# A six-cell attention stage in one kernel: pairing heads in the value product, output weights reordered in DRAM, input normalised in place

## The chip, the cores and the metric

The kernel runs on one core of one Trainium2 chip. Its time is the device time of one execution in microseconds (us): median 3191.99 us of three runs (3191.54 to 3194.13). The profiled execution took 3187.25 us, of which the span from first to last instruction is 3185.5 us, at a mean granted TensorE clock of 0.981 of full speed.

## The reference, cut to what matters

The reference is a chain of six residual layers on x of shape (64, 64, 256), that is 4096 tokens in 64 sequences of 64 tokens. Only the third layer, here called the cell stage, is changed. For the normalised input and for each of six nodes c it computes

```
nodes = {-1: inputs}
for c in range(6):
    q = ew[c, 0] * (nodes[c - 1]   @ We[eq] + be[eq])
    k = ew[c, 1] * (nodes[in_k]    @ We[ek] + be[ek])
    v = ew[c, 2] * (nodes[in_v]    @ We[ev] + be[ev])
    o = _mha(q, k, v, Wq[c], Wk[c], Wv[c], Wo[c])      # 8 heads of 32, softmax over the 64 tokens of a sequence
    nodes[c] = act_w[c] * o + q
out = _layernorm(nodes[5], ln_g, ln_b)                  # added to x
```

`_mha` projects q, k and v with 256x256 matrices, splits them into 8 heads of 32 columns, and multiplies the joined heads by Wo.

## The kernel before, in words

`build` runs the stages one after the other: masked attention, wide attention, the cell stage (`stage_cell`, about 1650 to 2733 us of the span), attention over a context, a scan, a feed-forward stage. Each stage gives every engine (PE, ACT, DVE, POOL, SP) its own list of instructions, written by hand, and semaphores join the lists. Nothing is scheduled at run time: each engine works through its list in order.

The cell stage has two parts.

*Preparation* (1650 to about 1717 us). Edge matrix and projection matrix of every node are multiplied once, because `(x @ We) @ Wq` is `x @ (We @ Wq)`. SP loads raw matrices (`load_raw`, L1939) into buffers that the main part uses later: even nodes into `prob`, odd ones into `probT` and `v`. For each of the 18 pairs (node c, f = q, k or v) PE transposes We (L2015), ACT copies it out (L2260), PE computes the bias column (L2022: four products of 128x128 by one column), then the fused matrix (L2030), and DVE scales it (L2438). SP waits for a node's last product before it loads the raw matrices two nodes ahead (L1957), and stores finished sets to DRAM (L1962). ACT loads the first edge and output matrix at n = 4 (`load_own`, L2243).

*Main part.* Tokens are worked on in blocks of 512; a round handles two blocks, X = 0 and 1, and there are four rounds (`rounds`, L1926: the first and last are written out, the middle two are a loop). A round has 12 slots: nodes c = 0 to 5 for X = 0 and 1. So the stage has 48 slots. A slot of PE's list (`body`, L2187) is: half of the q edge product (`add_edge`, L2133), turning the later two heads' probabilities (L2116), the other half, the value product `attend` (L2144), the next node's k projection (L2059), the output product `add_output` (L2155), turning the next slot's first two heads' probabilities (L2108), v projection (L2082), q projection (L2059), scores (L2097). In the slots of c = 5 the k projection is replaced by transposing the next round's input (`turn_input`, L2048), and the projections follow later. ACT copies results out of PSUM, applies exp; DVE finds maxima, sums and divisions, and makes the low parts for the split products (fp32r products are made three times, high by high, high by low, low by high).

`attend` (L2136) before: heads are numbered hf*4 + r, hf = 0 or 1, r = 0 to 3. Partitions 0 to 63 of `probT` hold the keys of the heads of hf = 0, partitions 64 to 127 those of hf = 1, and `v` is stored the same way: [128, X, s, b, 128 columns]. For each of the 8 sequences of a block (s, b), each hf and each r there is one fp32 product: 64 keys by 32 value columns as stationary operand, 64 query columns as moving operand. That is 64 products, in the array tiles of 64 rows by 32 columns. Results of hf go to bank `ring[hf]`, and the semaphore `attended` is raised for hf = 0 and hf = 1 after the last sequence. ACT then writes the high part of `oT` (L2353) and DVE the low part (L2537, a helper at L2419), one bank after the other; `add_output` waits for the first bank's low part, makes six products, waits for the second's (L2152).

`normalise` (L2407) waits for the input block in `x_ln`, makes statistics (DVE, L102), reciprocal roots (POOL, L114) and writes the normalised block into `xn[X]` (L130). One buffer `x_ln` serves all blocks; SP loads the next one when the last was read (L1979). POOL does nothing else in the stage than the roots. PE's two records for one fp32 product are both called MATMUL in the trace; an fp32r product or a transpose has one.

Of the kernel before, what the change touches and what calls it, by code (L numbers as in the profile page):

```python
# [1736 lines left out]
def stage_cell(nc, mem, const, x_in, ew, act_w, W_e, b_e, W_q, W_k, W_v, W_o, ln_g, ln_b, x_out):  # L1737
# [49 lines left out]
    set_dram = nc.dram_tensor("cell_weights", (NODES, P, 3 * MAT), F32, kind="Internal").ap()  # L1787
    w_stage = mem.sb("w_stage", [P, SET])
# [11 lines left out]
    x_ln = mem.sb("x_ln", [P, SUB, D])  # L1800
# [4 lines left out]
    v = mem.sb("v", [P, 2, SUB, 2, P])  # L1805
# [22 lines left out]
    set_loaded = mem.sem("set_loaded")  # L1828
    set_hi = mem.sem("set_hi")
# [11 lines left out]
    x_loaded = mem.sem("x_loaded")  # L1841
# [42 lines left out]

    def set_number(i, c):

        return i * NODES + c + 1
# [29 lines left out]

    def attention(i, c, X):

        return i * (2 * NODES) + 2 * c + X  # L1920
# [17 lines left out]
    def _(sp):  # L1938
# [25 lines left out]
        sp.wait_ge(norm.xn_ready, 1)  # L1964
        sp.dma_start(x_ln[:, :, :], block_rows(x_in[BLK:2 * BLK, :])).then_inc(x_loaded, 16)

        def body(i, last):
            for X in range(2):
                if not isinstance(i, int) or i >= 1:

                    sp.wait_ge(y_stored[X], i * 16)
                elif X == 0:

                    sp.wait_ge(stage_stored[1], STORED)
                sp.dma_start(x_res[:, X], block_rows(x_in[rows((i * 2 + X) * BLK, BLK), :])).then_inc(res_loaded[X], 16)
            if not last:
                for X in range(2):

                    sp.wait_ge(norm.xn_ready, (i + 1) * 2 + X)  # L1979
                    sp.dma_start(x_ln[:, :, :], block_rows(x_in[rows(((i + 1) * 2 + X) * BLK, BLK), :])).then_inc(x_loaded, 16)  # L1980
# [3 lines left out]
    @block.gpsimd  # L1984
    def _(pool):
        for X in range(2):
            norm.gpsimd_rstd(pool, X)

        def body(i, last):
            for X in range(2):  # L1990
                if not last:
                    norm.gpsimd_rstd(pool, (i + 1) * 2 + X)
            for X in range(2):
                last_norm.gpsimd_rstd(pool, i * 2 + X)

        rounds(pool, body)

    @block.tensor
    def _(pe):
# [6 lines left out]
        for c in range(NODES):  # L2006
            for f in range(3):
# [11 lines left out]
                for oh in range(DH):  # L2019
                    at = n * DH + oh  # L2020
                    for mh in range(DH):
                        mm = pe.matmul(prep_banks[3][:, at:at + 1], raw_w(c, RAW_W + f)[:, mh, oh * P:(oh + 1) * P],  # L2022
                                       be[:, mh, edge[c][f]:edge[c][f] + 1], start=(mh == 0), stop=(mh == DH - 1))
# [218 lines left out]
    def _(act):  # L2242
        def load_own(c):  # L2243

            for at, w in ((EDGE_AT, W_e[edge[c][0]]), (OUT_AT, W_o[c])):
                act.dma_start(w_stage[:, at:at + MAT].rearrange("p (h o) -> p h o", h=DH), w.rearrange("(h p) o -> p h o", p=P)).then_inc(set_loaded, 16)
# [64 lines left out]
        act.wait_ge(stage_stored[1], STORED)  # L2311
        copy_v(DH, 0)
# [93 lines left out]
    def _(dve):  # L2406
        def normalise(blk, X, turned):  # L2407
            dve.wait_ge(x_loaded, (blk + 1) * 16)
            norm.vector_stats(dve, blk, x_ln)
# [3 lines left out]
            norm.vector_apply(dve, blk, x_ln, False, xn[:, X])  # L2413
# [108 lines left out]
        def body(i, last):  # L2522
            for c, X in slots():
# [34 lines left out]
                if c in (3, 4) and X == 0 and not last:  # L2558
                    Y = c - 3

                    turned = Y * 6 + DH if isinstance(i, int) and i == 0 else proj_at(i, NODES - 1, Y) - PROJ_ROUND + DH
                    normalise((i + 1) * 2 + Y, Y, turned)
# [803 lines left out]
```

## Time and profile before

| | |
|---|---|
| Median of 3 runs | 3191.99 us |
| Profiled execution | 3187.25 us (span 3185.5 us) |
| PE busy, whole span | 3017.8 us (95%) |
| DVE / ACT / POOL busy | 2186.4 (69%) / 2009.2 (63%) / 941.1 (30%) us |
| Cell stage | about 1650 to 2733 us of the span |

The profile's page names busy shares, and the trace answers questions on a stretch, on a line, on waits. "Busy" counts the time in which at least one record of the engine is open; matmuls are pipelined, so their records overlap, and the mean duration of one is not what one costs. What one costs is read from the starts: the start of a group of instructions to the start of the next group on the engine.

### The profile page before, as it was taken

To read this page: it belongs to the slowest core of one execution; us is meant where nothing else is said; L and a number is where in the kernel's file an instruction comes from. 1 tells how busy PE (TensorE), PEld (TensorE's weight loads), DVE (VectorE), ACT (ScalarE), POOL (GpSimd) and SP (SyncE) were. 2 spreads that over 40 slices of the span, in tenths; PEclk is the share of its full clock that TensorE was granted. 3 is DMA by queue.
4 is the path that set the end of the run, shared out by engine and by line. 5 is a ranking of instruction groups with operands and counts; after the bars stand their busy time and mean duration, and the time that the engine had idled before them with its cause. 6 is when DMAs were issued, how large, how long until landed. Compare 5 with 4: busy or idle time off the path is not lost. (4 is left out here: it accounts for less than half of the span.)

```text
span 3185.5 us, 88343 instructions
## 1 busy us (share of the span) xinstructions
PE 3017.8 (95%) x34369; PEld 2466.6 (77%) x34369; DVE 2186.4 (69%) x5188; ACT 2009.2 (63%) x3697; POOL 941.1 (30%) x812
## 2 busy tenths in 40 slices
PE   8999999979999999999979999999999999799999
PEld 7888888857877877877868888788788787564798
DVE  5777777766666666666644788778778877567543
ACT  5777777757767767677743677676666766332444
POOL 3444444337656555555630000000000000111210
PEclk9999999989999999999989999999999999899899
DMA  2111111237888888888885111111111110552000
GB/s 86 47 46 46 46 46 46 57 52 128 151 141 150 151 137 146 152 145 148 156 188 173 35 42 49 55 42 49 56 42 42 54 36 19 179 163 77 7 21 27
DMA packets 643036, 273.37 MB, mean 86 GB/s; under 512 B 549387, under 2 KB 617952, under 8 KB 642736
## 3 DMA queue, kind: packets, MB, share of 16 engines
q1 hardware_dynamic: 613168, 225.13, 33.6%
q10 hardware_dynamic: 29568, 44.05, 4.2%
q8 instruction: 212, 3.47, 0.5%
q14 instruction: 88, 0.72, 0.1%
HBM read 113.37 MB, written 21.50 MB: 42 GB/s over the span
## 5 line engine op out<-in xcount | busy, mean ns | idle before, releaser
L1310 POOL TENSOR_TENSOR front_parts<-wide_prob,front_parts 128x1024 f16<-128x1024 f32 x256 | 549.1, 2146 | 377.5 <-ACT front_parts L1536 318.6
L1629 DVE TENSOR_REDUCE wide_row_max<-wide_score 128x1 f32<-128x1024 f32 x256 | 312.6, 1221 | 167.4 <-PE wide_score L1348 166.5
L1348 PE MATMUL wide_score<-wide_kT,wide_qT 128*128 128x512 f32 x1536 | 414.3, 405 | 4.9 <-ACT wide_prob L1524 3.3
L1524 ACT ACTIVATE wide_prob<-wide_score,wide_neg_max 128x1024 f32<-128x1024 f32 x256 | 285.2, 1114 | 157.3 <-DVE wide_neg_max L1632 151.0
L886 ACT ACTIVATE mask_prob<-mask_prob,mask_row_min 128x256 f32<-128x256 f32 x512 | 232.0, 503 | 161.7 <-DVE mask_row_min L966 161.7
L1348 PEld LDWEIGHTS wide_score<-wide_kT,wide_qT 128*128 128x128 f32 x1536 | 277.5, 190 | 66.0 <-issue 8.9
L1536 ACT ACTIVATE front_parts<-wide_prob 128x1024 f16<-128x1024 f32 x256 | 269.8, 1054 | 16.8 <-ACT wide_prob L1524 8.3
L2472 DVE TENSOR_REDUCE cell_row_max<-cell_score 128x8 f32<-128x512 f32 x192 | 131.0, 682 | 148.5 <-PE cell_score L2097 146.6
L117 POOL TENSOR_TENSOR cell_var_eps<-cell_mean_var,const_eps 128x4 f32<-128x4 f32 x8 | 1.6, 202 | 651.9 <-DVE cell_mean_var L111 651.9
L1364 PE MATMUL wide_turn<-front_probT,wide_v 128*128 128x256 f16 x1536 | 189.5, 273 | 2.5 <-DMA front_probT<-front_parts 2.5
L1364 PE MATMUL wide_pv<-front_probT,wide_v 128*128 128x256 f16 x1536 | 189.9, 273 | 0.5 <-DMA front_probT<-front_parts 0.5
L966 DVE CUSTOM_DVE_ANT_0 mask_prob<-mask_score,mask_shut 128x256 f32<-128x256 f32 x512 | 188.0, 419 | 0.0
L1364 PEld LDWEIGHTS wide_turn<-front_probT,wide_v 128*128 128x128 f16 x1536 | 140.6, 98 | 50.0 <-issue 35.6
L1364 PEld LDWEIGHTS wide_pv<-front_probT,wide_v 128*128 128x128 f16 x1536 | 140.4, 98 | 47.3 <-issue 32.6
L2133 PE MATMUL cell_acc<-cell_node,cell_w 128*128 128x512 f32 x576 | 159.8, 413 | 13.2 <-issue 7.0
L2300 ACT ACTIVATE cell_v<-cell_score 64x256 f32<-64x256 f32 x384 | 145.5, 379 | 35.6 <-PE cell_score L2082 25.5
L752 PE MATMUL mask_turn<-const_ident,mask_prob 128*128 128x128 f32 x1024 | 157.2, 276 | 9.7 <-ACT mask_probT L894 9.4
L1623 DVE SCALAR_TENSOR_TENSOR front_x_all<-wide_misc,wide_inv_sum,front_x_all 128x256 f32<-128x256 f32 (+1 forms) x256 | 112.0, 478 | 68.9 <-PE wide_misc L1375 68.9
L2082 PE MATMUL cell_score<-cell_w,cell_node 128*128 128x256 f32 x1152 | 151.3, 288 | 5.5 <-DVE cell_node L2419 4.0
L2155 PE MATMUL cell_acc<-cell_oT,cell_w 128*128 128x512 f32 x576 | 145.7, 402 | 10.8 <-DVE cell_oT L2419 10.8
L2082 PEld LDWEIGHTS cell_score<-cell_w,cell_node 128*128 128x128 f32 x1152 | 142.6, 193 | 9.4 <-issue 5.7
L2059 PE MATMUL cell_score<-cell_node,cell_w 128*128 128x512 f32 x576 | 147.1, 402 | 1.7 <-DVE cell_prob L2475 1.7
(364 smaller groups left out, 6845.6 us busy)
## 6 DMA issues: line engine op xcount, KB each, us to landing
cell_w_stage<-cell_weights ACTq DMA_DIRECT2D x24, 768.0 KB, 6.1
mask_ctx<-in_ctx SPq DMA_DIRECT2D x32, 512.0 KB, 3.9
ctx_ctx<-in_ctx SPq DMA_DIRECT2D x32, 512.0 KB, 4.2
mask_mask<-in_mask_BxS_ik SPq DMA_DIRECT2D x32, 256.0 KB, 4.0
front_probT<-front_parts SPq DMA_TRANSPOSE x512, 3.2
cell_w_stage<-in_L_ffn_We ACTq DMA_DIRECT2D x24, 256.0 KB, 2.7
cell_w_stage<-in_L_ffn_Wo ACTq DMA_DIRECT2D x24, 256.0 KB, 3.1
front_x_all<-in_x SPq DMA_DIRECT2D x32, 128.0 KB, 2.0
```

The costliest lines, as they stand in the source:

```text
L752: mm = pe.transpose(turn[:, (i * KT + kt) * P:(i * KT + kt + 1) * P], prob[:, b, s * 2 + i, kt * P:(kt + 1) * P], ident[:, :])
L886: ins = act.activation(prob[:, b, p, :], prob[:, b, p, :], ACT.Exp, bias=row_min[:, b, p:p + 1], scale=-1.0)
L966: ins = dve.tensor_tensor_reduce(prob[:, b, p, :], score[p % ROW][:, p // ROW * CTX:(p // ROW + 1) * CTX], shut[:, k, b].rearrange("p t r ...
L1310: pool.tensor_tensor(parts[:, s % 2, LO, :], prob[:, s % 2, :], parts[:, s % 2, HI, :], ALU.subtract).then_inc(part_lo, 1)
L1348: mm = pe.matmul(score[:, s % 2, half * 512:(half + 1) * 512], qT[:, u_par, a, s * P:(s + 1) * P], kT[:, par, b, half * 512:(half + 1) * 5 ...
L1364: mm = pe.matmul(pv_banks[hf][:, :], v[:, par, a, kb, :], probT[:, u_par, hf, :, b, kb, :], start=(kb == 0 and i == 0), stop=(kb == KB - 1 ...
L1524: act.activation(prob[:, s % 2, :], score[:, s % 2, :], ACT.Exp, bias=neg_max[:, s % 2:s % 2 + 1], scale=SHARP, accum_out=row_sum[:, u_par ...
L1536: act.activation(parts[:, s % 2, HI, :], prob[:, s % 2, :], ACT.Copy).then_inc(part_hi, 1)
L1629: dve.tensor_reduce(row_max[:, one], score[:, s % 2, :], AX.X, ALU.max).then_inc(max_found, 1)
L2059: mm = pe.matmul(dst[:, :], weight(a, fused_at(f), ih, half(oh)), src[:, b, ih, :], start=(j == 0 and ih == 0), stop=(j == 2 and ih == DH ...
L2082: mm = pe.matmul(score[2 + pair][:, s * D:(s + 1) * D], v_src[:, a, ih, half(2 * pair + s)], weight(b, fused_at(2), ih, slice(0, D)), star ...
L2133: pe.matmul(acc[oh][:, :], weight(a_, EDGE_AT, ih, half(oh)), src[:, b_, ih, :], start=(j == 0 and ih == 0), stop=False)
```

## The change

- `attend` makes one product for two heads, r of hf = 0 and r of hf = 1: 128 keys (partitions 0 to 127, both halves) by 64 value columns, 64 query columns. `v` gets 256 columns per sequence, in blocks of 64 for each r: 32 columns of hf = 0, then 32 of hf = 1. In the rows of one half the columns of the other are zero. There are 32 products, in array tiles of 128 rows by 64 columns. r = 0, 1 go to `ring[0]`, r = 2, 3 to `ring[1]`; all of bank 0 comes first, and `attended` is raised in the middle and at the end.
- POOL clears the zero places of `v` by four memsets, each waiting for the one before, once the last raw matrix in `v` has been used; ACT's first copy into `v` waits for them.
- The rows of `oT` now have another order. `W_o` is copied in DRAM to `out_dram` in that order, by 24 DMAs from DRAM to DRAM (`regroup_out`), 4 of them before the raw loads of node 1 and 20 behind them, in SP's list. `load_own` reads `out_dram`. The v bias columns are made in the new order, by 16 products of 32 columns instead of 4 of 128, for each of the 6 nodes.
- `x_ln` is gone: blocks are loaded into `xn[X]` and normalised there. The load of a round waits until PE has turned the block that was there.

```diff
-    v = mem.sb("v", [P, 2, SUB, 2, P])
+    v = mem.sb("v", [P, 2, SUB, 2, ROW * DH * DIM])
...
+    def own_half(t, hf):
+        return t.rearrange("p s (r a d) -> p s r a d", a=DH, d=DIM)[:, :, :, hf, :]
...
-        sp.dma_start(x_ln[:, :, :], block_rows(x_in[0:BLK, :])).then_inc(x_loaded, 16)
+        sp.dma_start(xn[:, 0], block_rows(x_in[0:BLK, :])).then_inc(x_loaded[0], 16)
+        def regroup_out(c):
+            w = W_o[c].rearrange("(a j r d) o -> r a d j o", a=DH, j=2, r=2)
+            for r in range(2):
+                for a in range(DH):
+                    sp.dma_start(out_dram[c][rows((r * DH + a) * DIM, DIM)].rearrange("p (j o) -> p j o", j=2), w[r, a])\
+                        .then_inc(out_turned[min(c, 1)], 16)
+        regroup_out(0)
         for f in range(3):
             load_raw(1, f)
+        for c in range(1, NODES):
+            regroup_out(c)
...
+        norm.gpsimd_rstd(pool, 0)
+        pool.wait_ge(fused_ready, 3 * NODES)
+        pool.wait_ge(norm.rstd_ready, 1)
         for X in range(2):
-            norm.gpsimd_rstd(pool, X)
+            for hf in range(DH):
+                if X + hf:
+                    pool.wait_ge(v_cleared, X * DH + hf)
+                pool.memset(own_half(v[hf * S:(hf + 1) * S, X].rearrange("p s b d -> p (s b) d"), 1 - hf), 0.0).then_inc(v_cleared, 1)
+        pool.wait_ge(v_cleared, 2 * DH)
+        norm.gpsimd_rstd(pool, 1)
...
+                        for n_, (r, hf) in enumerate((r, hf) for r in range(2) for hf in range(DH)):
+                            col = hf * P + oh * S + r * DIM
+                            pe.matmul(prep_banks[3][n_ * DIM:(n_ + 1) * DIM, at:at + 1], raw_w(c, RAW_W + f)[:, mh, col:col + DIM], b_col, **end)
...
-            for s in range(SUB):
-                for b in range(2):
-                    tok = slice(s * P + b * S, s * P + (b + 1) * S)
-                    for hf in range(DH):
-                        keys = slice(hf * S, (hf + 1) * S)
-                        for r in range(ROW):
-                            mm = pe.matmul(ring[hf][r * DIM:(r + 1) * DIM, tok], v[keys, X, s, b, r * DIM:(r + 1) * DIM],
-                                           probT[keys, r, tok], start=True, stop=True)
-                        if s == SUB - 1 and b == 1:
-                            mm.then_inc(attended, 1)
+            for bank in range(2):
+                for s in range(SUB):
+                    for b in range(2):
+                        tok = slice(s * P + b * S, s * P + (b + 1) * S)
+                        for half_bank in range(2):
+                            r = bank * 2 + half_bank
+                            mm = pe.matmul(ring[bank][half_bank * S:(half_bank + 1) * S, tok], v[:, X, s, b, r * S:(r + 1) * S],
+                                           probT[:, r, tok], start=True, stop=True)
+                mm.then_inc(attended, 1)
...
+                act.wait_ge(out_turned[0], 16 * 2 * DH)
                 load_own(0)
...
-                        ins = act.activation(v[hf * S:(hf + 1) * S, X, 2 * pair:2 * pair + 2, b, :],
-                                             src[b * S:(b + 1) * S, :, hf * P:(hf + 1) * P], ACT.Copy)
+                        ins = act.activation(own_half(v[hf * S:(hf + 1) * S, X, 2 * pair:2 * pair + 2, b, :], hf),
+                                             src[b * S:(b + 1) * S, :, hf * P:(hf + 1) * P].rearrange("p s (r d) -> p s r d", d=DIM), ACT.Copy)
...
+        act.wait_ge(v_cleared, 2 * DH)
+        act.wait_ge(out_turned[1], 16 * 2 * DH * (NODES - 1))
         copy_v(DH, 0)
...
-            norm.vector_stats(dve, blk, x_ln)
+            norm.vector_stats(dve, blk, xn[:, X])
```

## Rows read from the trace of the kernel before

**Rows 1.** Windows of the preparation and the main part; the columns are explained below.
```profile
core 0: us, PE busy (x) PEld busy (x) DVE busy (x) ACT busy (x) POOL busy (x), PEclk, DMA share, GB/s
1650.00:1720.00 70.00, 59.74 (x366) 54.31 (x367) 22.04 (x62) 12.45 (x20) 1.22 (x2) 0.91 0.68 220
1750.00:2733.00 983.00, 928.10 (x16264) 773.84 (x16262) 763.84 (x1306) 658.22 (x1221) 16.95 (x28) 0.99 0.13 43
```
**Rows 2.** Waits of PE after 1740 us: us in total, times, longest.
```profile
PE cell_acc L2155 <- DVE cell_oT L2419: 10.8, 10, 1.5
PE cell_score L2097 <- ACT cell_qT L2292: 7.2, 21, 1.0
PE cell_score L2059 <- DVE cell_prob L2475: 1.7, 2, 0.9
```
**Rows 3.** Timeline of PE, part of a slot: start us, us open, instruction, records.
```profile
2266.32 1.62 PE L2133 MATMUL cell_acc<-cell_node,cell_w 128*128 128x512 f32 x6
2267.86 1.48 PE L2144 MATMUL cell_ring<-cell_probT,cell_v 64*32 64x64 f32 x128
2269.28 1.67 PE L2059 MATMUL cell_score<-cell_node,cell_w 128*128 128x512 f32 x6
2270.85 3.05 PE L2155 MATMUL cell_acc<-cell_oT,cell_w 128*128 128x512 f32 x12
```
**Rows 4.** Timeline of PE, masked attention: array tiles of 128 by 32.
```profile
33.33 0.64 PE L770 MATMUL mask_heads<-mask_probT,mask_v 128*32 128x128 f32 x16
33.79 0.62 PE L770 MATMUL mask_heads<-mask_probT,mask_ones 128*32 128x128 f32 x16
34.34 0.66 PE L752 MATMUL mask_turn<-const_ident,mask_prob 128*128 128x128 f32 x4
```
**Rows 5.** Timeline of PE, context attention: array tiles of 128 by 64.
```profile
2750.94 1.09 PE L2711 MATMUL ctx_out_ps<-ctx_ctx,ctx_probT 128*64 128x256 f32 x8
2751.86 1.08 PE L2689 MATMUL ctx_score<-ctx_ctxT,ctx_xnT 128*64 128x256 f32 x8
2752.87 0.44 PE L2700 MATMUL ctx_probT_ps<-const_ident,ctx_prob 128*128 128x128 f32 x2
```
**Rows 6.** Timeline of PE, one step of the preparation.
```profile
1665.49 0.60 PE L2015 MATMUL cell_ring<-const_ident,cell_prob 128*128 128x128 f32 x4
1665.93 0.95 PE L2022 MATMUL cell_acc<-cell_be,cell_prob 128*128 128x1 f32 x8
1666.78 1.99 PE L2030 MATMUL cell_score<-cell_prob,cell_z 128*128 128x256 f32 x8
1668.61 0.60 PE L2015 MATMUL cell_ring<-const_ident,cell_probT 128*128 128x128 f32 x4
```
**Rows 7.** Timeline of ACT in the same step.
```profile
1666.13 0.60 ACT L2260 ACTIVATE cell_z<-cell_ring 128x512 f32<-128x512 f32 x1 [2.52 <-PE cell_ring L2015]
```
**Rows 8.** Timeline of PE, a slot of c = 5, X = 0.
```profile
2194.94 1.48 PE L2144 MATMUL cell_ring<-cell_probT,cell_v 64*32 64x64 f32 x128
2196.35 1.09 PE L2048 MATMUL cell_score<-const_ident,cell_xn 128*128 128x128 f32 x8
2198.92 3.06 PE L2155 MATMUL cell_acc<-cell_oT,cell_w 128*128 128x512 f32 x12 [1.48 <-DVE cell_oT L2419]
```
**Rows 9.** Timeline of DVE in the same slot.
```profile
2197.52 0.69 DVE L2475 TENSOR_TENSOR cell_prob<-cell_score,cell_row_max 128x512 f32<-128x512 f32 x1
2198.13 1.40 DVE L2419 SCALAR_TENSOR_TENSOR cell_oT<-cell_ring,cell_fused_bias,cell_oT 128x512 fp32r<-128x512 f32 x2
```
**Rows 10.** Timeline of SP's DMA queue: the issues before and after its wait.
```profile
1659.12 0.64 SPq L1953 DMA_DIRECT2D cell_b_row<-in_L_ffn_ln_b  x1
1668.80 0.38 SPq L1941 DMA_DIRECT2D cell_prob<-in_L_ffn_We  x1
```
**Rows 11.** DMA issues: count, KB each, median us from issue to landing.
```profile
cell_prob<-in_L_ffn_We SPq DMA_DIRECT2D x9, 256.0 KB, 4.1
```
**Rows 12.** Timeline of PE: where node 2's first raw matrix is used.
```profile
1677.96 0.60 PE L2015 MATMUL cell_ring<-const_ident,cell_prob 128*128 128x128 f32 x4
```
**Rows 13.** POOL by line: the group nearest to a memset (busy us, mean ns).
```profile
L3180 POOL TENSOR_TENSOR tail_x_all<-tail_x_all,tail_out_bias 128x1024 f32 (+1 forms) x8 | 19.1, 2391 | 13.4 <-DVE ffn_xn L130 13.4
```
**Rows 14.** Timeline of ACT: the first copies into v.
```profile
1725.65 1.55 ACT L2300 ACTIVATE cell_v<-cell_score 64x256 f32<-64x256 f32 x4 [2.65 <-PE cell_score L2082]
```

In Rows 1 the numbers of a row are the stretch, its length, then busy us and (x records) of each engine, the granted TensorE clock, the busy share of the DMA engines, and what they moved. In a timeline a number in brackets at the end is the idle time before the instruction and what ended it.

More of the change, by code:

```diff
@@ L1787, in stage_cell @@
     set_dram = nc.dram_tensor("cell_weights", (NODES, P, 3 * MAT), F32, kind="Internal").ap()
+    out_dram = nc.dram_tensor("cell_out_weights", (NODES, P, MAT), F32, kind="Internal").ap()
     w_stage = mem.sb("w_stage", [P, SET])
@@ L1828, in stage_cell @@
     set_loaded = mem.sem("set_loaded")
+    out_turned = [mem.sem(f"out_turned{i}") for i in range(2)]
+    v_cleared = mem.sem("v_cleared")
     set_hi = mem.sem("set_hi")
@@ L1840, in stage_cell @@
     proj_copied = mem.sem("proj_copied")
-    x_loaded = mem.sem("x_loaded")
+    x_loaded = [mem.sem(f"x_loaded{i}") for i in range(2)]
     res_loaded = [mem.sem(f"res_loaded{i}") for i in range(2)]
@@ L1916, in proj_at, with turned_at @@
         return i * PROJ_ROUND + PROJ_AHEAD + (2 * c + X) * PROJ_SLOT + (X * (PROJ_LAST - PROJ_SLOT) if c == NODES - 1 else 0)
+    def turned_at(i, X):
+        return X * 6 + DH if isinstance(i, int) and i == 0 else proj_at(i, NODES - 1, X) - PROJ_ROUND + DH
     def attention(i, c, X):
@@ L1977, in body @@
                 for X in range(2):
-                    sp.wait_ge(norm.xn_ready, (i + 1) * 2 + X)
-                    sp.dma_start(x_ln[:, :, :], block_rows(x_in[rows(((i + 1) * 2 + X) * BLK, BLK), :])).then_inc(x_loaded, 16)
+                    sp.wait_ge(proj_ready, turned_at(i, X))
+                    sp.dma_start(xn[:, X], block_rows(x_in[rows(((i + 1) * 2 + X) * BLK, BLK), :])).then_inc(x_loaded[X], 16)
         rounds(sp, body)
@@ L2021, in _ @@
                     for mh in range(DH):
-                        mm = pe.matmul(prep_banks[3][:, at:at + 1], raw_w(c, RAW_W + f)[:, mh, oh * P:(oh + 1) * P],
-                                       be[:, mh, edge[c][f]:edge[c][f] + 1], start=(mh == 0), stop=(mh == DH - 1))
+                        end = {"start": mh == 0, "stop": mh == DH - 1}
+                        b_col = be[:, mh, edge[c][f]:edge[c][f] + 1]
+                        if f < 2:
+                            pe.matmul(prep_banks[3][:, at:at + 1], raw_w(c, RAW_W + f)[:, mh, oh * P:(oh + 1) * P], b_col, **end)
+                            continue
+                        for n_, (r, hf) in enumerate((r, hf) for r in range(2) for hf in range(DH)):
+                            col = hf * P + oh * S + r * DIM
+                            pe.matmul(prep_banks[3][n_ * DIM:(n_ + 1) * DIM, at:at + 1], raw_w(c, RAW_W + f)[:, mh, col:col + DIM], b_col, **end)
                 pe.wait_ge(we_copied, n + 1)
@@ L2243, in load_own @@
         def load_own(c):
-            for at, w in ((EDGE_AT, W_e[edge[c][0]]), (OUT_AT, W_o[c])):
-                act.dma_start(w_stage[:, at:at + MAT].rearrange("p (h o) -> p h o", h=DH), w.rearrange("(h p) o -> p h o", p=P)).then_inc(set_loaded, 16)
+            act.dma_start(w_stage[:, EDGE_AT:EDGE_AT + MAT].rearrange("p (h o) -> p h o", h=DH), W_e[edge[c][0]].rearrange("(h p) o -> p h o", p=P))\
+                .then_inc(set_loaded, 16)
+            act.dma_start(w_stage[:, OUT_AT:OUT_AT + MAT], out_dram[c]).then_inc(set_loaded, 16)
         act.wait_ge(be_ready, 1)
@@ L2407, in normalise @@
         def normalise(blk, X, turned):
-            dve.wait_ge(x_loaded, (blk + 1) * 16)
-            norm.vector_stats(dve, blk, x_ln)
+            dve.wait_ge(x_loaded[X], (blk - X) * 8 + 16)
+            norm.vector_stats(dve, blk, xn[:, X])
             if turned is not None:
                 dve.wait_ge(proj_ready, turned)
-            norm.vector_apply(dve, blk, x_ln, False, xn[:, X])
+            norm.vector_apply(dve, blk, xn[:, X], False, xn[:, X])
         def low(dst, src, hi, bias=None):
@@ L2559, in body @@
                     Y = c - 3
-                    turned = Y * 6 + DH if isinstance(i, int) and i == 0 else proj_at(i, NODES - 1, Y) - PROJ_ROUND + DH
-                    normalise((i + 1) * 2 + Y, Y, turned)
+                    normalise((i + 1) * 2 + Y, Y, turned_at(i, Y))
                 if c == NODES - 1:
```

4 lines of the change are left out of this document (1 added, 3 removed).

## The prediction

> **What bounds the kernel now.** First the busy time by stretch. In the main part of the cell stage PE is busy for 928.1 of 983 us (94%) at a granted clock of 0.99, DVE for 763.8 (78%), ACT for 658.2 (67%) and the DMA engines for 0.13 [rows 1]. So PE's list sets the time, and what the change does to `attend` counts in full unless PE has a wait behind it. Second the waits of PE: few and short. The longest sum is 10.8 us in 10 waits of the output product for the low part of `oT` [rows 2]. Third the timeline of a slot, for what a group costs from start to start. `attend` starts at 2267.86 and the k projection behind it at 2269.28: 1.42 us for 64 products, 128 records [rows 3]. There are 48 of these, 68 us in all.
>
> **The value product.** Half as many products, each with twice the rows and twice the stationary columns. The question is whether PE pays per product or per moving column in an array tile. In tiles of 64 by 32 the array holds 8 tiles, in tiles of 128 by 64 it holds 2. Before, each tile gets 128/8 = 16 records of 64 moving columns; after, 64/2 = 32 records of 64 columns. So the multiplied zeros are paid for by lost tiles: the columns that a tile must stream double.
>
> What does a column cost? Three fp32 rows. Tiles of 128 by 32 (4 of them): 32 records of 128 columns from 33.33 to 34.34, 8 in each tile, 1.01 us, so 126 ns a record, 0.99 ns a column [rows 4]. Tiles of 128 by 64 (2 of them): 16 records of 256 columns from 2750.94 to 2752.87, 8 in each, 1.93 us, 241 ns a record, 0.94 ns a column [rows 5]. The whole array: 8 records of 256 columns from 1666.78 to 1668.61, 229 ns, 0.89 ns a column [rows 6]. The first two contain changes of tiling, the third has nearly none. With 0.89: 32 x 64 x 0.89 = 1.82 us; I add 0.03 for the change of tiling at both ends, which the 1.42 also contains in part, and take 1.85 us. That is 0.43 us more than 1.42. The old form streams only 16 x 64 x 0.89 = 0.91 us in a tile, so its 1.42 is not set by streaming: its 128 records come 11 ns apart, and something per record, feeding or loading, sets it.
>
> Bounds of the new form. Below: rows 5 less 0.2 us for its two changes of tiling (my estimate) gives 0.84 ns a column, 1.73 us, +0.31. Above: if the loads of stationary columns don't overlap between the two tiles. Eight loads of 128 columns with one moving column take 1665.93 to 1666.78, 0.85 us, 106 ns a load, 0.83 ns a stationary column [rows 6]. 64 loads of 64 columns one after the other are then 64 x 53 ns = 3.4 us, +2.0. I stay near the streaming value: in the old form each row half takes 64 loads of 32 columns in 1.42 us, 22 ns each, less than the 27 ns by that rate, so loads of different column tiles do overlap there [rows 3].
>
> The Trainium skill ("TensorEngine Tiling (Array Packing)", Tiling Modes) lists 8 tiles for 64x32 and 2 for 128x64, and says that different tiles load and multiply in parallel. By that rule nothing is gained from pairing: the sum is the one above. The 11 ns per record in rows 3 agree that more than one tile works at a time.
>
> 48 x 0.43 = +20.6 us. What is given back: waits behind `attend` whose end does not hang on it. In the slot at 2194.94 PE waits 1.48 us for the low part of `oT`, but DVE starts that part at 2198.13, directly behind its subtraction for the next slot's scores [rows 8, 9]; `attend` may end 0.43 later at no cost. I count the 10 such waits and the 2 for the subtraction itself [rows 2]: 12 x 0.43 = -5.2. Bank 0 is now ready 0.9 us before the end of `attend`. In an ordinary slot that buys nothing, for the output product follows its predecessor without a bracketed wait [rows 3]; in the last two slots, where nothing lies between, up to 0.9 us each: -1.5. The 21 waits for ACT's q copy [rows 2] lie behind the projections and stay. ACT's copies into `v` keep their number and size, only with 32-column pieces: 0, hidden by ACT's idle third; if each grew by a tenth, those q waits would grow by some 0.3 us each, 6 us.
>
> **The preparation.** PE sets it too. One step is 1665.49 to 1668.61, 3.12 us [rows 6], 18 steps. *Bias columns:* in 6 steps, 16 products of 32 columns for 4 of 128, 32 records for 8. At the 32 ns a record of rows 4 that is 1.0 us for 0.85, and two changes of tiling. If shorter, nothing is won: PE waits for ACT's copy, which ends at 1666.73 [rows 7]. 0 to +0.4 each; I take +0.15, +1. *Reordering W_o:* 24 more issues on SP at 0.38 to 0.64 us are 9 to 15 us. SP was idle from 1659.76 to 1668.80, 9.0 us [rows 10]. So node 2's loads start 0 to 6 us later. They had 9.2 us (1668.80 to 1677.96) and take 4.1 [rows 11, 12]: slack 5. The 1.6 MB, read and written, run in the same stretch, where the DMA engines are 0.68 busy [rows 1], in line before node 2's loads. No DRAM to DRAM transfer is in this trace; below 0, above: if it moved at half of the 220 GB/s, 14 us from 1660, then loads at 1674 + 4, nearly no delay, or some 4 us with queueing. I take +1. Node 1's loads are 4 issues (2 us) later, used from 1668.61 on; hidden. ACT's wait for the first four is over before n = 4. *Memsets:* 64 x 1024 elements each. Nearest: 128x1024 at 2.39 us [rows 13]; four are at most 9.6 us from 1716.4 on, until 1726.0, against the copy at 1725.65 [rows 14]; +0 to +0.4, I take 0. The second root waits for them on POOL, and its block is turned only at 1733. *Normalising in place:* same DVE instructions, loads issued a round ahead: 0.
>
> **Sum.** 20.6 - 5.2 - 1.5 + 1 + 1 = +15.9 us on the profiled execution's 3187.25 (span 3185.5): 3203. The median of the runs was 4.7 above that execution; on it the forecast is 3208.
>
> **Rivals.** *Products, not columns (ends faster).* If PE is fed at a fixed pace, the 11 ns a record of rows 3 hold for the new form, and `attend` takes 64 x 11 = 0.71 us: 48 x -0.71 = -34, with +2 of preparation 3160. For it: the old form does not stream at its limit. Against it: the 32 records of rows 4 come 32 ns apart and those of rows 5 121 ns, in tiles of 128 rows; there columns decide. It decides once a tile's 32 x 64 columns take less than 1.42 us, under 0.69 ns a column, which no fp32 row shows. *Loads in line.* 3.4 us per `attend`: +2.0 x 48 = +96, of which the 12 waits (12.5 us) are swallowed: +84 and 2, 3278. For it: 64 stationary columns per 64 moving ones is a ratio that no row with 128-row tiles has; against it the 22 ns above. The Trainium skill ("TensorE: Matmul & The Clock Gate", Part 3) says that a load overlaps products in flight only when the row group differs; with all 128 rows in each tile none does. That speaks for this rival, and for its 3278. Rows 4 don't bear it out strictly: 32 loads at 27 ns would be 0.85 us and streaming 8 x 128 x 0.89 another 0.91, and both fit in 1.01 us. Half way, 2.4 us, would give +37, 3229. *Swallowed.* Streaming at 1.73 us, and the early bank and the waits take half of it back: 48 x 0.31 = 14.9, less 9, so +6, 3198. *The preparation grows.* If DRAM to DRAM is slow enough that nodes 2 to 5 each wait 3 us: +12 more, 3220.
>
> **How the numbers follow.** A run of this kernel can't tell less than 0.2% (6.4 us) from nothing. Forecast 0.58, swallowed 0.12 (half of it within 0.2%), preparation 0.08, loads in line or half way 0.14, products 0.08. Faster 0.09, same 0.10, slower 0.81. The range goes from 3196 (1.73 us and most waits used) to 3238 (half way and the preparation); the likeliest's own is 3200 to 3218.
>
> **What would show it.** `attend` from start to the next start 1.8 to 1.9 us, with 64 records of 128*64; 0.7 means products, over 2.3 loads in line. The bracketed waits of the output product shorter by 0.4 where they stand on DVE. A step of the preparation at 3.12 us with no bracket on a raw matrix. The stages behind unchanged. The forecast is wrong if the main part doesn't grow by 10 to 20 us.

## The result and the profile after

The changed kernel takes 3202.22 us (median of 10 runs, 3198.99 to 3207.20), the kernel before 3192.07 us (10 runs, 3189.04 to 3196.32). The ratio is 1.0032, interval [1.0022, 1.0042]: 10.2 us slower. The forecast was 3208 and the range 3196 to 3238. The profiled execution took 3201.79 us (span 3199.8, granted clock 0.981 as before). It lies 0.4 us under its median where the one of before lies 4.8 under its own, so the two traces differ by 14.5 us, the medians by 10.2.

The windows of preparation and main part, in the columns of [rows 1]:

```profile
1650.00:1720.00 70.00, 60.00 (x504) 52.64 (x505) 18.99 (x42) 12.44 (x20) 1.22 (x2) 0.88 0.71 232
1750.00:2733.00 983.00, 954.55 (x13314) 806.18 (x13314) 766.75 (x1296) 662.22 (x1220) 15.69 (x26) 0.99 0.13 42
```

In this window PE makes 2950 records fewer and is busy for 26 us more. Read between fixed marks of the two traces (first transpose of a raw matrix, first turn of the input, first transpose of the context stage), the preparation grew from 62.97 to 69.71 us, the main part from 1019.2 to 1029.1, and the stages behind stayed (446.7 and 446.7). The stages ahead, which the change does not touch, were 2.3 us shorter in the trace of after (the first transpose is at 1654.32 for 1656.65). So there are two places where time was lost, and they are read one after the other.

**The slot.** PE's timeline, the same part of a slot as [rows 3]:

```profile
2280.79 1.62 PE L2166 MATMUL cell_acc<-cell_node,cell_w 128*128 128x512 f32 x6
2282.34 2.08 PE L2177 MATMUL cell_ring<-cell_probT,cell_v 128*64 128x64 f32 x64
2284.35 1.66 PE L2092 MATMUL cell_score<-cell_node,cell_w 128*128 128x512 f32 x6
```

`attend` takes 2.01 us from start to next start instead of 1.42: +0.59 here, +0.60 as the median of the 48. Its 64 records start over 1.86 us; after the first ones they come 58 ns apart in each of the two tiles. That is 48 x 0.60 = 28.9 us gross. The main part grew by only 10.0 us, so about 19 us came back elsewhere. PE's waits after 1740 us (us in total, times, longest), against [rows 2]:

```profile
PE cell_acc L2187 <- DVE cell_oT L2455: 4.3, 6, 0.9
PE cell_score L2130 <- ACT cell_qT L2326: 3.9, 16, 0.3
```

Both are about half of before or less; the two waits for the subtraction are gone. The c = 5 slot of X = 0 that the prediction used, PE and then DVE, as in [rows 8, 9]:

```profile
2207.86 2.09 PE L2177 MATMUL cell_ring<-cell_probT,cell_v 128*64 128x64 f32 x64
2209.87 1.09 PE L2081 MATMUL cell_score<-const_ident,cell_xn 128*128 128x128 f32 x8
2211.84 2.36 PE L2187 MATMUL cell_acc<-cell_oT,cell_w 128*128 128x512 f32 x9 [0.87 <-DVE cell_oT L2455]
```

```profile
2210.44 0.69 DVE L2511 TENSOR_TENSOR cell_prob<-cell_score,cell_row_max 128x512 f32<-128x512 f32 x1
2211.05 1.40 DVE L2455 SCALAR_TENSOR_TENSOR cell_oT<-cell_ring,cell_fused_bias,cell_oT 128x512 fp32r<-128x512 f32 x2
```

The wait shrank from 1.48 to 0.87, by exactly what `attend` grew: DVE's low part still starts right behind its subtraction. From the start of `attend` to that of the output product it is 3.98 us in both kernels. Such a slot pays nothing. Group by group over the main part, with the idle time ahead of each group: `attend` itself (first to last record start) 64.2 to 90.9, +26.7; the output products -10.3; the scores -4.5; the projections -3.9; all else +2.0. Sum +10.0.

**The preparation.** PE at the first use of node 2, which was at 1677.96 without a bracket [rows 12]:

```profile
1679.88 0.94 PE L2042 MATMUL cell_ring<-const_ident,cell_prob 128*128 128x128 f32 x4 [4.14 <-DMA cell_prob<-in_L_ffn_Wq]
1680.62 1.70 PE L2052 MATMUL cell_acc<-cell_be,cell_prob 128*128 128x1 f32 x8
1682.19 3.76 PE L2063 MATMUL cell_score<-cell_prob,cell_z 128*128 128x256 f32 x8
1685.74 1.06 PE L2042 MATMUL cell_ring<-const_ident,cell_prob 128*128 128x128 f32 x4
```

SP's queue, against [rows 10]:

```profile
1652.97 2.60 SPq L1964 DMA_DIRECT2D cell_out_weights<-in_L_ffn_Wo  x4
1659.73 13.25 SPq L1964 DMA_DIRECT2D cell_out_weights<-in_L_ffn_Wo  x20
1674.13 0.43 SPq L1951 DMA_DIRECT2D cell_prob<-in_L_ffn_We  x1
```

The 20 copies hold SP for 13.25 us, 0.66 each. Node 2's loads are issued at 1674.13 instead of 1668.80, 5.3 us later. PE ran some 2 us earlier in this trace and came to node 2 at 1675.74, only 1.6 us behind that issue (9.2 before), and it stands idle for 4.14 us. It pays once more behind the wait: the granted clock in 1678 to 1690 is 0.72 (next row), it was 1.00 before, and the fused product is open for 3.76 us instead of 1.99. The first step takes 5.86 us, the second 3.64, for 3.12: +3.3. A wait of 0.71 us for DVE that node 2 had before is gone. Together that is 4.14 + 3.3 - 0.7 = 6.7. Node 3 and later nodes wait for no matrix.

```profile
1678.00:1690.00 12.00, 10.12 (x53) 8.87 (x57) 4.81 (x13) 1.19 (x2) 1.22 (x2) 0.72 1.02 363
```

The step with the new bias columns, as in [rows 6] (an f = 2 step), and the memsets:

```profile
1663.11 0.60 PE L2042 MATMUL cell_ring<-const_ident,cell_prob 128*128 128x128 f32 x4
1663.64 0.43 PE L2056 MATMUL cell_acc<-cell_be,cell_prob 128*32 128x1 f32 x32
1664.40 1.99 PE L2063 MATMUL cell_score<-cell_prob,cell_z 128*128 128x256 f32 x8 [0.33 <-ACT cell_z L2294]
1666.23 0.60 PE L2042 MATMUL cell_ring<-const_ident,cell_probT 128*128 128x128 f32 x4
```

```profile
1720.79 3.95 POOL L2012 MEMSET cell_v<- 64x1024 f32 x4 [41.01 <-PE cell_score L2063]
```

The step is 3.12 us, as before: 32 short records need less than the 8 wide loads did, and PE then waits 0.33 us for ACT's copy, as the prediction said. The four memsets end at 1724.74, more than 5 us ahead of ACT's first copy into `v` (1730.07).

### The profile page after: what moved, and what is told of

It reads as the page before. It is cut to its first block and busy times, and to the rows that moved or that the text cites. A ratio compares the mean times of both kernels' runs of the same rounds, so it can differ in the third digit from the quotient of the medians.

```text
span 3199.8 us, 82520 instructions
## 1 busy us (share of the span) xinstructions
PE 3045.5 (95%) x31441; PEld 2496.5 (78%) x31441; DVE 2192.0 (69%) x5188; ACT 2013.1 (63%) x3697; POOL 944.0 (30%) x816
## 5 line engine op out<-in xcount | busy, mean ns | idle before, releaser
L752 PEld LDWEIGHTS mask_turn<-const_ident,mask_prob 128*128 128x128 f32 x1024 | 116.3, 140 | 41.3 <-issue 29.7
```

What stands on the lines that cost most here:

```text
L752: mm = pe.transpose(turn[:, (i * KT + kt) * P:(i * KT + kt + 1) * P], prob[:, b, s * 2 + i, kt * P:(kt + 1) * P], ident[:, :])
```

## The experiments

Two questions: where the rest of `attend`'s cost went, and what sets its pace. Where a kernel was executed once only, its trace is read and not its time.

### The reordering of W_o

e1_no_reorder takes it out, with the waits on it, and reads `W_o` as it is (its rows do not fit the new order of `oT`).

```diff
-        regroup_out(0)
-        for c in range(1, NODES):
-            regroup_out(c)
-            act.dma_start(w_stage[:, OUT_AT:OUT_AT + MAT], out_dram[c])...
+            act.dma_start(w_stage[:, OUT_AT:OUT_AT + MAT]..., W_o[c].rearrange("(h p) o -> p h o", p=P))...
```

> The changed kernel without the 24 DMAs that reorder W_o in DRAM and without the waits on them; the output weights are read from W_o as before, so their rows stand in the wrong order (left out: the reordering). Theory (the DMAs cost about 6 us in the preparation, 4.1 us of it a wait of PE for node 2's raw matrix and the rest a slower clock behind that wait): preparation from the first transpose to the first input turn back from 69.7 to 63 us, time 3202 - 6 = 3196, +0.1% on before. Rival (the reordering is hidden, and the 6 us are the bias columns and the memsets): preparation stays near 69 us, time 3202.

e2_reorder_spread keeps all 24 copies, but issues those of nodes 1 to 5 one node at a time, behind the raw loads and the store of a set:

```diff
-        for c in range(1, NODES):
-            regroup_out(c)
...
             sp.dma_start(set_dram[(c - 3) % NODES], made_of(c - 2)).then_inc(stage_stored[c % 2], 16)
+            if c < NODES + 1:
+                regroup_out(c - 1)
```

> The changed kernel with the same 24 DMAs, but those of nodes 1 to 5 issued one node at a time behind the raw loads and the set store of nodes 2 to 6, where SP would wait. Theory (place in SP's list counts, not the traffic): preparation near 63 us, no wait of PE on a raw matrix, 3196. Rival (the traffic itself, DRAM to DRAM beside loads at a DMA share of 0.7, costs): waits of PE on raw matrices remain, spread over nodes, preparation 66 to 70 us, 3199 to 3203.

Measured: e1 3198.93 us (12 runs), ratio to before 1.0021 [1.0010, 1.0032]; e2 3197.83 us (12 runs), 1.0017 [1.0007, 1.0027]. The preparation is 66.0 us in e1, 63.08 in e2 (before 62.97). In e1 PE waits for no matrix either, but its first steps were at a low granted clock for longer (0.79 in 1663 to 1678, 1.00 in the kernel after), so its 66.0 lies between its two expectations. e2 met its first one. SP's queue and PE in e2:

```profile
1669.53 0.38 SPq L1951 DMA_DIRECT2D cell_prob<-in_L_ffn_We  x1
1673.03 3.64 SPq L1964 DMA_DIRECT2D cell_out_weights<-in_L_ffn_Wo  x4
```

```profile
1676.86 1.99 PE L2063 MATMUL cell_score<-cell_v,cell_z 128*128 128x256 f32 x8 [0.33 <-ACT cell_z L2294]
1678.69 0.60 PE L2042 MATMUL cell_ring<-const_ident,cell_prob 128*128 128x128 f32 x4
```

The same traffic, issued later, costs nothing: what costs is the place in SP's list. It is worth 0.0015 of the ratio, 4.4 us by the medians (6.6 in the trace). The intervals of the ratios overlap a little; the wait in the trace is what speaks for it.

The wait is not there in every execution. Seven traces have this list of SP (after, e3, e5, e6, e8, e9, e11). Six show the wait, of 2.0 to 4.6 us. In e3, SP's queue and PE:

```profile
1675.93 0.43 SPq L1951 DMA_DIRECT2D cell_prob<-in_L_ffn_We  x1
```

```profile
1682.10 0.66 PE L2042 MATMUL cell_ring<-const_ident,cell_prob 128*128 128x128 f32 x4
```

The loads are nearly as late as in the others, but PE's clock was low for longer at the start (0.79 in 1663 to 1678, as in e1). PE reached node 2 only 6.2 us behind the issue and waited for nothing. The preparation is 66.1 us, as in e1 without any copies. So the copies cost nothing in one trace and 6.7 us in the trace pair. In these two it went with the clock: the sooner PE has its full clock, the sooner it stands at node 2.

What is left of e2, 0.0017 or 5 us, is the main part; e2 is the best form of the change that was run, and still slower than before.

### The early bank

e3_signal_end raises `attended` for both banks at the end, everything else as after:

```diff
-                mm.then_inc(attended, 1)
+            mm.then_inc(attended, 2)
```

> The changed kernel with both increments of the semaphore behind the value product given at its end, so that bank 0 is no longer handed over in the middle. Theory A (most of the give-back of 19 us is waits that a longer value product swallows anyway, whatever is handed over early): +2 to +5 us on the changed kernel, 3204 to 3207. Theory B (the early bank gives most of it back: the output product's waits fell from 10.8 to 4.3 us, scores' from 7.2 to 3.9): +8 to +12 us, 3210 to 3214, and the waits of the output product on DVE back at 8 us or more.

Measured: 3207.32 us (6 runs), 1.0047 [1.0030, 1.0063]; main part 1037.1 us in its trace, +8.0 on after, +5.1 by the medians. Waits of PE:

```profile
PE cell_acc L2187 <- DVE cell_oT L2455: 8.3, 10, 1.6
PE cell_score L2130 <- ACT cell_qT L2326: 5.4, 18, 0.8
```

The prediction had said that in ordinary slots an early bank buys nothing and put 1.5 us on it. It buys 5 to 8, though the intervals of e3 and after overlap and two traces of the same main part can differ by 4 us (see e4). Slot by slot the growth over after is in those of c = 0 (+2.9 us in all) and c = 5 (+2.7), where the output product does stand on `oT`, and hardly in the other 32 (+0.9); the rest lies behind the last slot. So neither "1.5 us" nor "all that came back" holds: roughly a third of the 19 us is the early bank.

e10_old_bank_first gives the old products the same order, one bank before the other:

```diff
-            for s in range(SUB):
-                for b in range(2):
-                    tok = slice(s * P + b * S, s * P + (b + 1) * S)
-                    for hf in range(DH):
-                        keys = slice(hf * S, (hf + 1) * S)
+            for hf in range(DH):
+                keys = slice(hf * S, (hf + 1) * S)
+                for s in range(SUB):
+                    for b in range(2):
+                        tok = slice(s * P + b * S, s * P + (b + 1) * S)
...
-                        if s == SUB - 1 and b == 1:
-                            mm.then_inc(attended, 1)
+                mm.then_inc(attended, 1)
```

> The kernel before, same 64 products in tiles of 64 by 32, but all of hf = 0 first, then all of hf = 1, so that bank 0 is handed over in the middle of the value product, as the change does. Theory A (the 1.42 us of the old form are a pace of 17 to 20 ns per product, whatever rows it uses): still 1.42 us, and the early bank gives back what it gave the changed kernel, 5 to 8 us: 3185 to 3188, faster than both. Theory B (products in the same rows can't follow each other at that pace, 33 ns a product in one row half, so the two halves must take turns): 2.1 us inside, time 3200 or more less the early bank, 3195 to 3203.

Measured: 3196.87 us (12 runs), 1.0010 [0.9999, 1.0021], no clear change. PE, and its wait:

```profile
2161.67 1.89 PE L2144 MATMUL cell_ring<-cell_probT,cell_v 64*32 64x64 f32 x128
```

```profile
PE cell_acc L2154 <- DVE cell_oT L2418: 5.8, 7, 1.1
```

The waits of the output product fall nearly as with the change (10.8 to 5.8 us, for 4.3), but `attend` itself takes 1.67 us from first to last record start instead of 1.27: with one half of the rows at a time only 4 tiles are in play. The time is that of the second expectation, but its 2.1 us of `attend` are not. What follows is that the early bank cannot be had alone in this layout: six us of waits (5.0 of the output product, 1.1 of the scores) stand against 18 us of `attend`.

### In-place normalising

e4_in_place_only is the kernel before with `x_ln` removed and blocks loaded into `xn[X]`:

```diff
-            norm.vector_stats(dve, blk, x_ln)
+            norm.vector_stats(dve, blk, xn[:, X])
...
-            norm.vector_apply(dve, blk, x_ln, False, xn[:, X])
+            norm.vector_apply(dve, blk, xn[:, X], False, xn[:, X])
```

> The kernel before with only the third part of the change: blocks loaded into xn and normalised there, no x_ln. Theory: no part of the time, 3192 within 2 us. Rival (the reuse of one buffer was a hidden wait, or in-place writing slows DVE): 3 us or more either way, seen in the duration of the normalising instructions (409 ns before) or in the wait before the statistics.

Measured: 3191.94 us (12 runs), 0.9997 [0.9987, 1.0007]. Nothing, as said. Its main part is 1023.4 us in the trace against 1019.2 of the kernel before: two traces of equal kernels differ by 4 us here, so the 10.0 us of the trace pair is 6 to 10, and the 19 us that came back 19 to 23.

### What sets the pace of attend

Six runs, of one execution each, change one size of the products each. They leave part of the value product out or put it in the wrong place, so only the pace is read. e5 halves the moving columns (`few`, 32 of 64), e6 takes 48 stationary columns and e9 32 of 64, e7 is the kernel before with 32 moving columns:

```diff
-  mm = pe.matmul(ring[bank][half_bank * S:(half_bank + 1) * S, tok], v[:, X, s, b, r * S:(r + 1) * S], probT[:, r, tok], ...)
+  e5: mm = pe.matmul(ring[bank][half_bank * S:(half_bank + 1) * S, few], v[:, X, s, b, r * S:(r + 1) * S], probT[:, r, few], ...)
+  e6: mm = pe.matmul(ring[bank][half_bank * S:half_bank * S + 48, tok], v[:, X, s, b, r * S:r * S + 48], ...)
+  e9: mm = pe.matmul(ring[bank][half_bank * S:half_bank * S + DIM, tok], v[:, X, s, b, r * S:r * S + DIM], ...)
+  e7: mm = pe.matmul(ring[hf][r * DIM:(r + 1) * DIM, few], v[keys, X, s, b, r * DIM:(r + 1) * DIM], probT[keys, r, few], ...)
```

> The changed kernel, value product with 32 instead of 64 moving columns (left out: half of the query tokens). Start of the value product to the start of the next group is 2.02 us with 64 columns (1.42 in the old form). If streamed columns set it (59 ns for a record of 64 in each of two tiles): 1.0 to 1.1 us. If the loads of 64 stationary columns set it (53 ns each, two tiles side by side): unchanged at 1.8 to 2.0 us. If records at a fixed pace set it, unchanged too.

> The changed kernel, value product with 48 instead of 64 stationary columns (left out: half of the odd half's columns). If streamed columns set its 2.02 us: unchanged. If the loads of stationary columns set it: 1.6 us.

> The kernel before, value product with 32 instead of 64 moving columns (left out: half of the query tokens). If its 1.42 us are a pace per record (128 records at 11 ns): unchanged at 1.4. If streaming sets part of it (0.91 us by 57 ns a record in 8 tiles): 1.1 us or less.

> The changed kernel, value products of 128 rows by 32 stationary columns, 64 moving (left out: the odd half's columns, whose results keep what the bank held). 64 stationary columns took 59 ns a product, 48 took 56. Theory A (a fixed pace of some 50 ns for full-height tiles with 0.1 to 0.2 ns a stationary column): 52 ns a product, 1.65 us inside. Theory B (loads of stationary columns): 30 ns, 1.0 us.

e8 puts all products into one column tile; e11 doubles the moving columns to 128:

```diff
+  e8:  mm = pe.matmul(ring[bank][0:S, tok], v[:, X, s, b, r * S:(r + 1) * S], ...)
+  e11: mm = pe.matmul(ring[bank][half_bank * S:(half_bank + 1) * S, half(s)], v[:, X, s, b, r * S:(r + 1) * S], probT[:, r, half(s)], ...)
```

> The changed kernel, all 32 value products written to partitions 0 to 63 of their bank, so all in one column tile of 128 by 64 (left out: the heads of the upper half bank, which are overwritten). In the changed kernel a product starts every 59 ns, two tiles in turn, and neither half the moving columns nor three quarters of the stationary ones changed that much. Theory A (the pace belongs to the array's rows: in a tile of all 128 rows nothing of the next product's load goes beside it, whichever columns it has): unchanged, 1.9 us inside the value product. Theory B (each tile has a pace of 118 ns and the two run side by side): twice as long, 3.7 us.

> The changed kernel, each of the 32 value products with 128 instead of 64 moving columns (both sequences of a half block with the values of one; the second overwrites the first, so the results of one sequence in two are wrong). Theory A (pace of 59 ns a product, and two tiles streaming 128 columns in 107 ns a record, two records a product, two tiles side by side, would be 107 ns a product): 3.4 us inside, so streaming takes over between 64 and 128 columns. Theory B (a product's two records stream side by side): still 1.9 us.

PE's `attend`, one slot each, in the order e5, e6, e9, e8, e11, e7:

```profile
2284.64 2.06 PE L2177 MATMUL cell_ring<-cell_probT,cell_v 128*64 128x32 f32 x64
```

```profile
2283.14 1.99 PE L2177 MATMUL cell_ring<-cell_probT,cell_v 128*48 128x64 f32 x64
```

```profile
2281.53 1.98 PE L2177 MATMUL cell_ring<-cell_probT,cell_v 128*32 128x64 f32 x64
```

```profile
2327.52 3.94 PE L2177 MATMUL cell_ring<-cell_probT,cell_v 128*64 128x64 f32 x64
```

```profile
2320.34 3.71 PE L2177 MATMUL cell_ring<-cell_probT,cell_v 128*64 128x128 f32 x64
```

```profile
2078.25 1.29 PE L2144 MATMUL cell_ring<-cell_probT,cell_v 64*32 64x32 f32 x128
```

The median over the groups, from the first to the last record's start, and the usual time from one record to the next in the same tile. The last two rows are the products for the bias columns, new and old: their lines are shown above and in [rows 6].

| Kernel | tiles | stationary x moving | us | records per tile | ns from record to record in a tile | us of the run |
|---|---|---|---|---|---|---|
| after | 2 | 64 x 64 | 1.86 | 32 | 58 | 3202.2 |
| e5 | 2 | 64 x 32 | 1.84 | 32 | 58 | 3204.5 |
| e6 | 2 | 48 x 64 | 1.78 | 32 | 56 | 3199.5 |
| e9 | 2 | 32 x 64 | 1.76 | 32 | 56 | 3194.8 |
| e8 | 1 | 64 x 64 | 3.72 | 64 | 58 | 3286.5 |
| e11 | 2 | 64 x 128 | 3.44 | 32 | 109 | 3275.8 |
| before | 8 | 32 x 64 | 1.27 | 16 | 80 (mean) | 3192.1 |
| e10 | 4, then 4 | 32 x 64 | 1.67 | 16 + 16 | 56 | 3196.9 |
| e7 | 8 | 32 x 32 | 1.10 | 16 | 69 (mean) | 3189.1 |
| after, L2056 | 4 | 32 x 1 | 0.26 | 8 | 32 | |
| before, L2022 | 1 | 128 x 1 | 0.70 | 8 | 112 | |

e8 shows that the pace belongs to the tile: in one tile everything takes twice as long, and two tiles run side by side. Within a tile two costs compete, and they overlap.

- *Loading the stationary columns.* With half the moving columns (e5) the step stays at 58 ns. A stream at 0.89 ns a column would take 0.9 us in all, and it takes 1.84. So at 64 x 64 the moving columns do not set the pace. With one moving column a step takes 32 ns for 32 stationary columns and 112 ns for 128, and 58 ns for 64 lies between.
- *Streaming the moving columns.* With 48 stationary columns (e6) the step falls to 56 ns and stays there with 32 (e9) and in e10. So there the stationary columns do not set the pace, and 64 moving ones do. 128 moving columns (e11) take 109 ns, 0.85 ns a column, near the 0.89 of [rows 6].

One rule fits all these rows: a record holds its tile for the longer of the two, 32, 58 or 112 ns for 32, 64 or 128 stationary columns, and 56 or 109 ns for 64 or 128 moving ones. A fixed time per record does not fit: 32 x 1 takes 32 ns and not 58. Nor does the sum of the two, which for 64 x 64 would be over 110 ns. The new form sits where both are nearly equal, and that is why halving either one alone gains at most 0.10 us.

In the old form with 8 tiles the tile is not the limit: 16 x 56 = 0.90 us of its 1.27. e7 shows that its time falls with fewer moving columns, to 1.10, which lay between its two expectations; what sets that pace stays open.

The Trainium skill ("TensorEngine Tiling (Array Packing)", Tiling Modes) says that different tiles load and multiply in parallel; e8 against after, 3.72 us in one tile and 1.86 in two, agrees. The Trainium skill ("TensorE: Matmul & The Clock Gate", Part 3) lets a load overlap products in flight only where the row group differs. The trace does not agree: the two tiles of `attend` have the same rows and still halve the time, and in e8's one tile a record takes 58 ns, where load and stream in turn would take over 110.

### A longer attend without the pairing

e12_old_longer takes the kernel before and makes the first 32 products twice, so that only the length of `attend` changes:

```diff
-            for s in range(SUB):
+            for n, s in enumerate((0, 1, *range(SUB))):
```

> The kernel before, each value product with its first 32 of 64 products made twice (same results, 96 products), both banks still handed over at the end, nothing else changed. At the old pace of 20 ns a product this adds 0.6 us to each of 48 value products, 29 to 31 us of PE's work, as the change does, with more instead of fewer instructions. Theory A (about half of such a lengthening is swallowed by waits for DVE and ACT that don't hang on the value product): +12 to +18 us, 3204 to 3210, and the waits of scores for ACT's q copy fall from 7 to 8 us to 4 to 5. Theory B (the give-back of the changed kernel came from its fewer PE instructions or its other edits): +24 to +30 us, 3216 to 3222.

Measured: 3281.68 us (5 runs), 1.0283 [1.0259, 1.0307], 86 us slower. Both expectations failed. Waits of PE, and one slot:

```profile
PE cell_ring L2144 <- issue: 40.7, 26, 2.9
PE cell_score L2097 <- issue: 8.2, 6, 2.7
PE cell_score L2097 <- ACT cell_qT L2292: 4.4, 18, 0.3
PE cell_acc L2155 <- DVE cell_oT L2419: 3.2, 4, 1.5
```

```profile
2201.29 1.48 PE L2144 MATMUL cell_ring<-cell_probT,cell_v 64*32 64x64 f32 x129
2203.74 0.85 PE L2144 MATMUL cell_ring<-cell_probT,cell_v 64*32 64x64 f32 x63 [0.96 <-issue]
```

An undisturbed `attend` is 1.90 us, +0.63, which over 48 slots is 30 us. Most of the rest are gaps inside `attend` in which PE waits for nothing but its next instruction. The old slot is near what its instruction supply gives, and the kernel before has small gaps too, here 0.94 us inside its 32nd `attend`:

```profile
2389.83 0.45 PE L2144 MATMUL cell_ring<-cell_probT,cell_v 64*32 64x64 f32 x30 [0.94 <-issue]
```

Three of its 48 `attend` groups take 1.93 to 2.37 us instead of 1.27, and such gaps add 2.9 us to the 48. After the change half of these products are gone, and no `attend` has such a gap; only the last one is longer, by 1.5 us, at a granted clock of 0.56. Elsewhere in the main part PE has waits that end in "issue" too. With the gaps inside `attend` they are 10.0 to 17.6 us in four traces with the old products (e10, before 12.8, e4 14.1, e7) and 8.3 to 9.6 in seven with the new ones. So the change gives some of this back, but the trace pair alone cannot say how much.

The waits on DVE and ACT did fall in e12, from 10.8 to 3.2 and from 7.2 to 4.4 us, with no early bank in it, so a later end of `attend` alone can swallow them. How much of that is the longer `attend` and how much the gaps, this run does not separate.

## Why the prediction was right, and where it was not

Direction and main mechanism held: pairing heads halves the products and costs the array tiles, `attend` gets longer, and PE is the bound, so the kernel is slower. The time lay 5.8 us under the forecast, inside the range. But several terms were off and in part cancel, so that the total came this close is partly luck. It lies nearer to the rival "swallowed" (3198) than to the forecast (3208).

- **`attend`, +0.43 forecast, +0.60 measured (28.9 us for 20.6).** Its sign, 1.8 to 1.9 us, was missed with 2.01. "32 x 64 x 0.89 = 1.82" was nearly right in size, 1.86. It was right for a reason the prediction did not give: it let moving columns alone decide within a tile, but the step of 58 ns is that of loading 64 stationary columns, and streaming 64 columns takes 56 beside it (e5, e9). The prediction had the load rate, 53 ns for 64 columns, and used it only for loads in line over both tiles. With 32 moving columns its sum would have been off by half. The mis-sized term is the ends: from the last record's start to the next group it is 0.15 us both before and after, and the forecast allowed 0.03. That is 0.12 of the 0.16 us missed.
- **What is given back, 6.7 forecast, 19 to 23 measured.** This step failed. "In an ordinary slot that buys nothing" is true of most slots but not of those of c = 0; there and at c = 5 the early bank gives nearly all of its 5 to 8 us (e3), for 1.5 forecast. "The 21 waits for ACT's q copy stay" is false: 7.2 to 3.9 us. That they hang on the projections alone is refuted by e3, where they are 5.4; e12 (4.4) suggests that a later `attend` gives ACT time as well. And stalls for instructions were not foreseen at all; in the trace pair they are 12.8 and 9.2 us. By the rows of waits of the pair: output product 6.5, q copy 3.3, subtraction 1.7, v projection 1.3, instructions 3.6, less 1.0 for a last `attend` at a low clock that cost more than before; that is 15.4. How the remainder divides is open.
- **Main part.** Forecast 13.9; 10.0 in the trace pair, about 5 by the medians (e2). The forecast's own condition, 10 to 20 us, is at its lower edge by the one and missed by the other.
- **Preparation, +2 forecast, 4.4 by the medians and 6.7 in the trace pair.** The rival "the preparation grows" holds for node 2 alone, once, not for four nodes at 3 us, and in e3's trace not even there. The failed step is the slack of 5 us behind "24 more issues at 0.38 to 0.64 us": they take 0.66 (the 0.64 of [rows 10] is that of a small row, the 0.38 that of a raw matrix), so the 20 copies fill SP's idle time and 5.3 us more, and the sum took PE's arrival as fixed. PE came 2.2 us earlier in this trace (1675.74 for 1677.96), and the first loads that it needed were there only 5.8 us after their issue, not 4.1. The low granted clock behind the wait, another 3.3 us, was in no term. The sign "a step at 3.12 us with no bracket on a raw matrix" was missed at node 2 and held elsewhere.
- **At nothing, rightly:** bias columns (the +1 is 0), memsets (3.95 us for a bound of 9.6), the in-place block (e4).
- **Rivals.** "Products, not columns" (0.71 us, 3160) is refuted by the 2.01 us and by e8. "Loads in line" (3.4 us, 3278) is refuted by the 2.01 us as well, but half of it was right: loads do set the pace, in each tile by itself. With one tile (e8) they are in line, and that run took 3.72 us and 3286. "Swallowed" (3198) was the nearest rival: much of the cost is given back, though from a larger gross than it took.

Open: what paces 8 tiles, what limits PE's supply of instructions in e12, and the split of the give-back between swallowed waits and instruction supply.

## What to carry to other kernels

For small fp32 products count the records per array tile and multiply by the longer of two times, loading (32, 58, 112 ns for 32, 64, 128 stationary columns) and streaming (56, 109 ns for 64, 128 moving ones). Packing zeros to halve the products cost more than it saved here, because it cut the tiles from 8 to 2. Longer work ahead of a wait is partly free: before charging 48 times, look which slots wait for another engine behind it, and in which order results are handed over (that order was worth 5 to 8 us here). DMA issues set into an idle stretch of an in-order queue push every load behind them; put them behind the loads that someone waits for (e2). Two traces of one kernel can disagree on such a wait (after and e3), so look at more than one.

## What the runs showed of the hardware

- A tile takes one fp32 record per 58 ns with 64 stationary columns, whether 64 or 32 are moving (after, e5, and e8 in one tile); per 56 ns with 48 or 32 stationary and 64 moving (e6, e9, e10); per 109 ns with 128 moving (e11); per 32 ns with 32 stationary and 1 moving (L2056 of after); per 112 ns with 128 stationary and 1 moving (L2022 of before). Tiles run side by side: 1.86 us in two, 3.72 in one.
- 96 instead of 64 small products in a slot of some 20 us made PE stand 40.7 us for its own instructions (e12), with no other engine named in these waits.
- A DRAM to DRAM copy of 64 KB in pieces of 1 KB held SP's queue for 0.66 us from one to the next (20 in 13.25 us); a load of 256 KB (L1951 of after, 36 loads) 0.47 in the middle, with single ones up to 1.39.
- In the trace of after a wait of 4.14 us on PE was followed by a stretch of granted clock 0.72, in which two steps took 3.3 us more than at the full clock.
